# Gated cross attention and a quantised feed-forward: transposes from TensorE to the DMA queue, down projections two tiles late, and a written-out, reordered instruction stream

## The chip, the cores and the metric

One core of one Trainium2 chip. Times are device microseconds of one execution; lower is better. TensorE is written PE (matmuls) and PEld (its weight loads), VectorE is DVE, ScalarE is ACT, GpSimd is POOL, SyncE is SP.

## The reference

`x` is 8 batches of 256 x 512, the context likewise. Two stages follow one another:

```
xn = layernorm(x)                                   # rows of 512
theta = theta_w @ ctx + b;  phi = phi_w @ xn + b;  g = (g_w @ xn) + b     # latent 128
p  = softmax(theta^T phi)                           # 512 x 512 for each batch
tx = g applied to p;  h = relu(layernorm(tx over latent and time) * gamma + beta)
x  = x + tanh(g_xattn) * (out_w @ h + out_b + ctx)
# second stage, rows of 512, hidden 2048, each input quantised to 8 bits by its row's maximum,
# each weight to -1, 0, 1 by its mean absolute value
y  = layernorm(x);  q(z) = quantise(rmsnorm(z))
h  = silu(q(y) @ w1^T) * (q(y) @ w2^T);  out = x + tanh(g_ffn) * (q(h) @ w3^T)
```

## The kernel before

**Attention stage.** One step for each batch `i`. On TensorE `project(i)` makes theta, phi and g (L938, L944, L952); then `values(i - 1)` turns the four 128-column quarters of the older batch's probabilities (four 128 x 128 transposes each, L986) and contracts each with g (L980), with the output projection of batch `i - 2` (L967) between the first quarters; then the four score quarters of batch `i` (L1032: three matmuls each, since theta and phi are kept as a high and a low part) and two small matmuls with a matrix of 1/128 that average over the partitions (L998, L1002). VectorE takes row maxima (L603), low parts (L616), the statistics of the next batch (L589, L594), gamma (L664), the layer norm (L634) and the output add (L642). ScalarE makes the high parts (L466, L469), copies g and the turned quarters out of PSUM (L475, L452), does exponentials (L496) and relu (L447). GpSimd normalises the input (L287, `x_norm`) and the probabilities (L297, `normalise`), makes x + tanh(gate) * (ctx + bias) (`residual`, L272 and L276), and takes inverse roots (L264).

Beside it the three weights of the second stage (4 MB each) are loaded, summed in absolute value on ScalarE (L423), scaled and rounded on GpSimd (L283) and cut to their sign on ScalarE (L442).

The order of one TensorE step, with a wait of the next step's theta for the exponentials of this one:

```
def step(i, s, turn, before=True, older=True, weight=None):
    project(i, s, turn)        # theta waits exp_done 4*i - 3, phi 4*i - 2
    ...
        values(i - 1, 1 - s, out_proj if older else None)
    for c in range(TC):
        ...                    # scores of quarter c, mean_mm after c == 1
        var_mm(i - 1)
```

**Second stage.** 16 row tiles of 128 rows, two to a pair. For a tile, `up(t, k, c)` for c = 0 to 3 multiplies the turned, quantised input with 512 columns of w1 and of w2 (8 matmuls, L1074) into one of two pairs of PSUM banks. ScalarE: silu (L515), square with a sum (L524). VectorE: product (`hmul`, L782), maximum (L787), then the scale (L792 to L809). GpSimd: inverse root, rounding and writing of 8-bit values as bf16 in two halves (L360, L364). TensorE turns them (`turn_h`, 16 transposes, L1089), ScalarE copies them (L530), and `down(t - 1)` (16 matmuls, L1104) stands behind the up projections of tile t. The input of the next pair is prepared in the same way (`prep_*`), turned by `turn_x` (8 transposes, L1009) in the middle of a down projection and copied (L436). VectorE adds the residual (L815), SP stores the tile (L240).

Every engine runs its own instruction list; semaphores join them. The middle of both stages is a hardware loop on each engine (`Fori`), two batches or two tiles a turn. Between the stages, `values(B - 1)` and what follows it for the last batch stand between the up projections of tiles 0 and 1.

## Time and profile before

| | us |
|---|---|
| median of 3 runs | 359.27 (357.31 to 360.0) |
| the profiled execution | 357.35 |
| its span, first to last instruction | 355.6 |
| TensorE busy | 319.7 (90%) |
| VectorE busy | 250.6 (70%) |
| ScalarE busy | 242.8 (68%) |
| GpSimd busy | 209.7 (59%) |
| mean granted TensorE clock | 0.986 |

A busy share is a mean over both stages; the same engine may be full in one and half idle in the other. Matmuls overlap in the records, so the pitch from start to start is what one costs.

### The profile page before, as it was taken

To read this page: it belongs to the slowest core of one execution; us is meant where nothing else is said; L and a number is where in the kernel's file an instruction comes from. 1 tells how busy PE (TensorE), PEld (TensorE's weight loads), DVE (VectorE), ACT (ScalarE), POOL (GpSimd) and SP (SyncE) were. 2 spreads that over 40 slices of the span, in tenths; PEclk is the share of its full clock that TensorE was granted. 3 is DMA by queue.
4 is the path that set the end of the run, shared out by engine and by line. 5 is a ranking of instruction groups with operands and counts; after the bars stand their busy time and mean duration, and the time that the engine had idled before them with its cause. 6 is when DMAs were issued, how large, how long until landed. Compare 5 with 4: busy or idle time off the path is not lost.

```text
span 355.6 us, 5790 instructions
## 1 busy us (share of the span) xinstructions
PE 319.7 (90%) x1614; PEld 173.9 (49%) x1638; DVE 250.6 (70%) x608; ACT 242.8 (68%) x439; POOL 209.7 (59%) x237
## 2 busy tenths in 40 slices
PE   0999899899989996696999999999999999999955
PEld 0665556555656464342454454545544555455532
DVE  1438656756675699448888798788887987887560
ACT  1296767979797864785766687577776776667621
POOL 3768927795779565702756637646567275563530
PEclk9999999999999999899999999999999999999988
DMA  7977902545400000000000000000000000000000
GB/s 246 397 301 289 405 23 113 189 167 191 163 0 0 0 4 0 0 2 0 0 3 30 29 29 23 6 29 29 29 0 29 29 29 0 29 30 31 24 35 29
DMA packets 11471, 26.39 MB, mean 74 GB/s; under 512 B 1088, under 2 KB 1984, under 8 KB 10432
## 3 DMA queue, kind: packets, MB, share of 16 engines
q1 hardware_dynamic: 10352, 25.82, 19.0%
q10 hardware_dynamic: 1104, 0.40, 0.4%
q8 instruction: 6, 0.10, 0.1%
q14 instruction: 9, 0.07, 0.1%
HBM read 22.02 MB, written 4.19 MB: 74 GB/s over the span
## 4 chain that ended last, share of the span: by engine, by line
PE 38%; issue 19%; ACT 15%; DVE 14%; POOL 11%; DMA 2%; POOLq 1%; ACTq 0%; DVEq 0%
PE bank L1074 12%; PE bank L1104 8%; ACT prob L496 5%; POOL prob L297 5%; PE bank L980 5%; ACT wq L442 4%; PE bank L986 4%; PE bank L967 3%; POOL stage L364 3%; DVE m L787 2%; DMA g_w<-g_wt_dram 2%; PE bank L1089 2%; ACT stage L515 2%; PE bank L938 2%; POOL stage L360 1%
## 5 line engine op out<-in xcount | busy, mean ns | idle before, releaser
L1074 PE MATMUL bank<-wq,stage 128*128 128x512 bf16 x495 | 114.5, 379 | 4.4 <-ACT prob L496 1.3
L1074 PEld LDWEIGHTS bank<-wq,stage 128*128 128x128 bf16 x512 | 49.2, 98 | 60.6 <-DVE x L642 2.1
L515 ACT ACTIVATE stage<-bank,s 128x512 f32<-128x512 f32 x64 | 44.2, 690 | 43.1 <-PE bank L1074 28.8
L782 DVE SCALAR_TENSOR_TENSOR stage<-bank,s,stage 128x512 f32<-128x512 f32 x64 | 47.9, 749 | 27.4 <-ACT stage L515 17.7
L1104 PE MATMUL bank<-wq,stage 128*128 128x512 bf16 x249 | 60.2, 387 | 0.7 <-ACT stage L530 0.3
L524 ACT ACTIVATE stage<-stage 128x512 f32<-128x512 f32 x64 | 40.2, 629 | 5.3 <-DVE stage L782 5.3
L360 POOL TENSOR_SCALAR stage<-stage,hsc 128x1024 f32<-128x1024 f32 (+1 forms) x31 | 34.9, 1138 | 14.5 <-DVE hsc L807 14.5
L787 DVE TENSOR_REDUCE m<-stage 128x1 f32<-128x512 f32 x64 | 41.8, 675 | 0.0
L1104 PEld LDWEIGHTS bank<-wq,stage 128*128 128x128 bf16 x256 | 25.0, 99 | 30.2 <-issue 2.8
L297 POOL TENSOR_SCALAR prob<-prob,rsum 128x512 f32<-128x512 f32 x32 | 24.6, 783 | 21.4 <-DVE rsum L669 21.4
L530 ACT COPY stage<-bank 128x1024 bf16<-128x1024 bf16 x32 | 31.0, 1015 | 6.8 <-PE bank L1089 6.6
L264 POOL TENSOR_TENSOR fsc<-fsc,neghalf 128x2 f32<-128x2 f32 x16 | 11.2, 700 | 37.5 <-DVE fsc L736 19.9
L980 PE MATMUL bank<-probT,gs 128*128 128x512 f32 x64 | 32.5, 611 | 0.3 <-ACT probT L452 0.3
L364 POOL TENSOR_SCALAR stage<-stage 128x1024 bf16<-128x1024 f32 (+1 forms) x31 | 32.1, 1054 | 0.2 <-POOL stage L360 0.2
L452 ACT COPY probT<-bank 128x512 f32<-128x512 f32 x32 | 18.5, 584 | 15.0 <-PE bank L986 14.9
L1032 PE MATMUL bank<-ph,th 128*128 128x512 f32 x96 | 28.1, 429 | 0.0
L938 PE MATMUL bank<-c_sb,theta_w 128*128 128x512 f32 x32 | 17.5, 673 | 11.1 <-DMA g_w<-g_wt_dram 8.4
L496 ACT ACTIVATE prob<-bank,nmax 128x512 f32<-128x512 f32 x32 | 21.6, 685 | 6.3 <-DVE nmax L603 6.3
L423 ACT ACTIVATE wq<-stage 128x1024 bf16<-128x1024 f32 x24 | 25.4, 1058 | 0.0
L283 POOL TENSOR_SCALAR stage<-stage,winv 128x2048 f32<-128x2048 f32 x12 | 23.6, 1979 | 2.3 <-DVE winv L611 2.3
L986 PEld LDWEIGHTS bank<-ident,prob 128*128 128x128 f32 x128 | 15.6, 143 | 18.8 <-issue 17.1
L986 PE MATMUL bank<-ident,prob 128*128 128x128 f32 x128 | 19.8, 280 | 5.1 <-POOL prob L297 3.9
(100 smaller groups left out, 522.5 us busy)
## 6 DMA issues: line engine op xcount, KB each, us to landing
x_sb<-x_dram SPq DMA_DIRECT2D x8, 512.0 KB, 5.8
c_sb<-ctx_in_dram SPq DMA_DIRECT2D x8, 512.0 KB, 6.7
stage<-w1t_dram SPq DMA_DIRECT2D x4, 1024.0 KB, 13.9
stage<-w2t_dram SPq DMA_DIRECT2D x4, 1024.0 KB, 11.1
stage<-w3t_dram SPq DMA_DIRECT2D x4, 1024.0 KB, 6.1
out_dram<-stage SPq DMA_DIRECT2D x16, 256.0 KB, 2.0
gam<-gamma_dram SPq DMA_DIRECT2D x1, 256.0 KB, 6.2
bet<-beta_dram SPq DMA_DIRECT2D x1, 256.0 KB, 6.4
```

The lines of the kernel that those rows point to most:

```text
L297: nc.gpsimd.tensor_scalar(prob[:, c], prob[:, c], rsum[:, c:c + 1], 1.0, ALU.mult, ALU.mult)\
L360: nc.gpsimd.tensor_scalar(part, part, hsc[:, 5:6], ROUND, ALU.mult, ALU.add).then_inc(pool_chain, 1)
L364: nc.gpsimd.tensor_scalar(hq[:, lo:hi], h_sb[k][:, lo:hi], -ROUND, 1.0, ALU.add, ALU.mult).then_inc(hq_ready, 1)
L496: nc.scalar.activation(prob[:, c], b_sc[c][:, :], ACT.Exp, bias=nmax[:, c:c + 1], accum_out=esum[:, c:c + 1]).then_inc(exp_done, 1)
L515: nc.scalar.activation(sil[:, c % 2], bank[:, :], ACT.Silu, scale=s12[:, 0, k:k + 1])\
L524: nc.scalar.activation(junk, h_sb[k][:, c * 512:(c + 1) * 512], ACT.Square, accum_out=ssq[:, c:c + 1]).then_inc(sq_done, 1)
L782: V.scalar_tensor_tensor(h_sb[k][:, c * 512:(c + 1) * 512], bank[:, :], s12[:, 1, k:k + 1], sil[:, c % 2], ALU.mult, ALU.mult).then_inc(hm ...
L787: link.inc(V.tensor_reduce(m4[:, c:c + 1], h_sb[k][:, c * 512:(c + 1) * 512], AX_X, ALU.max, apply_absolute_value=True))
L980: return mm(b_gt[:, :], gs[:, s, c * P:(c + 1) * P], probT[:, c], start=c == 0, stop=c == TC - 1)
L986: last_tr = tr(b_pt[c % 2][:, tc * P:(tc + 1) * P], prob[:, tc, c * P:(c + 1) * P], ident[:, :])
L1074: last = mm(bank[:, :], xT[:, (k * KI + q) * P:(k * KI + q + 1) * P], wq[:, at:at + 512], start=q == 0, stop=q == KI - 1)
L1104: last = mm(b_dn[:, :], hT_sb[:, q * P:(q + 1) * P], wq[:, at:at + T], start=q == 0, stop=q == KF - 1)
```

## The change

Nearly the whole file is rewritten; the arithmetic on the tensors stays.

- All loops are written out; the helper `wait_apart` is gone.
- **Transposes of the second stage.** `turn_x` and `turn_h` leave TensorE and its PSUM banks. SP issues a DMA transpose of the whole turned input of a pair (128 x 1024 bf16) and of each half of a tile's hidden values (128 x 1024 bf16 each). Only the last tile is still turned by TensorE and copied by ScalarE and VectorE.
- **Late down projections.** `down(t - 2)` stands behind the up projections of tile t, not `down(t - 1)`. Two buffers for the quantised and for the turned hidden values; up projections go round three pairs of banks in place of two.
- **Attention order.** See the TensorE list below. Quarters 0 and 1 of the scores stand ahead of the turns of the older batch, and its values, the output halves of batch i - 2 and the other score quarters alternate. The small means of batch i - 2 stand behind theta and phi. Probabilities have two buffers, the turned quarters two of one quarter each. On ScalarE the first copy of a turned quarter stands behind the first exponential, the second behind the second, relu behind that.
- **Who does what.** x is loaded straight into its result buffer `x2`. VectorE normalises the input (`x_norm`) and adds the gated context (`residual`), which were GpSimd's; GpSimd makes only tanh(gate) * (ctx + bias), in place.
- Weights are treated in 24 pieces of 1024 columns, six ScalarE slots in each batch; maxima and squares of the hidden values are two of 1024 columns a tile in place of four of 512.

```diff
-            step(0, 0, 1, before=False, older=False)
-            step(1, 1, 1, older=False)
-            with pe.Fori(1, B // 2 - 1) as j:
-                step(2 * j, 0, j + 1, weight=j - 1)
-                step(2 * j + 1, 1, j + 1, weight=j - 1)
+            for i in range(B):
+                theta(i)                     # waits exp_done 4*i - 1
+                if i >= 2:
+                    mean_mm(i - 2, {3: 0, 5: 1}.get(i))
+                phi(i)
+                if i >= 2:
+                    var_mm(i - 2)            # waits dev_ready
+                g(i)
+                if i in (2, 4, 7):
+                    weight_total({2: 0, 4: 1, 7: 2}[i], i)
+                scores(i, 0)
+                scores(i, 1)
+                if i >= 1:
+                    turn_p(i - 1, 0)
+                    turn_p(i - 1, 1)
+                    values(i - 1, 0)
+                if i >= 2:
+                    out_proj(i - 2, 0)
+                scores(i, 2)
+                if i >= 1:
+                    turn_p(i - 1, 2)
+                    values(i - 1, 1)
+                if i >= 2:
+                    out_proj(i - 2, 1)
+                scores(i, 3)
+                if i >= 1:
+                    turn_p(i - 1, 3)
+                    values(i - 1, 2)
+                    values(i - 1, 3)
...
-            def turn_h(t):
-                for half in range(2):
...
-                        last = tr(b_hT[half][:, :].bitcast(BF16)[:, n * P:(n + 1) * P], hq[:, at:at + P], identb[:, :])
...
+            def turn_h(t):
+                for half in range(2):
+                    sp.wait_ge(hq_ready, 2 * t + half + 1)
+                    if t >= 2 and half == 0:
+                        sp.wait_ge(dn_done, t - 1)
+                    lo, hi = half * HF, (half + 1) * HF
+                    sp.dma_start_transpose(hT[t % 2][:, lo:hi].rearrange("p (n r) -> p n r", r=P), hq[t % 2][:, lo:hi])\
+                        .then_inc(hT_loaded[t % 2][half], 16)
...
+            for t in range(1, NT):
+                turn_h(t - 1)
+                if t % 2 == 0 and t // 2 + 1 < NU:
+                    turn_x(t // 2 + 1)
+                if t >= 3:
+                    store(t - 3)
...
+            for t in range(2, NT):
+                for c in range(FC):
+                    up(t, c)
+                down(t - 2)
+            down(NT - 2)
```

VectorE's and ScalarE's lists in one batch of the new kernel, from i = 2 on (without the weights):

```
VectorE: tx_mean(i-2), sum_inverse(i-1), low_part theta, tx_dev(i-2), low_part phi, tx_gamma(i-2), tx_var(i-2),
         x_stats(i+1), tx_norm(i-2), row_max 0, row_max 1, residual(i), x_norm(i+1), add_out(i-2, 0),
         row_max 2, add_out(i-2, 1), row_max 3
ScalarE: slot 0, theta_high, slot 1, phi_high, slot 2, g_copy, exp 0, p_copy(i-1, 0), exp 1, p_copy(i-1, 1),
         relu(i-2), slot 3, p_copy(i-1, 2), slot 4, exp 2, p_copy(i-1, 3), slot 5, exp 3
```

## Rows read from the trace of the kernel before

**Rows 1.** the page: busy time of each engine (share of span, instructions).

```profile
PE 319.7 (90%) x1614; PEld 173.9 (49%) x1638; DVE 250.6 (70%) x608; ACT 242.8 (68%) x439; POOL 209.7 (59%) x237
```

**Rows 2.** busy time (count) in five stretches; last: granted clock, DMA share, GB/s.

```profile
8.42:32.94 24.52, 24.23 (x100) 15.47 (x101) 12.93 (x29) 14.06 (x29) 19.18 (x23) 1.00 0.82 320
32.94:120.94 88.00, 80.75 (x346) 49.28 (x346) 57.41 (x130) 73.67 (x129) 66.75 (x70) 1.00 0.36 138
120.94:178.40 57.46, 47.33 (x215) 25.14 (x219) 41.79 (x107) 38.52 (x65) 28.56 (x31) 0.97 0.00 1
178.40:340.00 161.60, 159.55 (x922) 80.27 (x941) 132.17 (x330) 113.35 (x214) 89.69 (x99) 1.00 0.06 23
340.00:355.60 15.60, 7.89 (x35) 3.70 (x34) 4.52 (x10) 1.93 (x2) 3.27 (x3) 0.78 0.09 34
```

**Rows 3.** TensorE's timeline, batch 4: start, duration, line, operation [idle before].

```profile
67.68 1.98 PE L938 MATMUL bank<-c_sb,theta_w 128*128 128x512 f32 x4 [0.75 <-ACT prob L496]
69.50 1.88 PE L944 MATMUL bank<-xn,phi_w 128*128 128x512 f32 x4
...
73.86 0.65 PE L986 MATMUL bank<-ident,prob 128*128 128x128 f32 x4 [0.69 <-POOL prob L297]
74.34 1.02 PE L967 MATMUL bank<-hn,out_w 128*128 128x512 f32 x2
75.20 0.60 PE L986 MATMUL bank<-ident,prob 128*128 128x128 f32 x4
...
80.49 1.95 PE L1032 MATMUL bank<-ph,th 128*128 128x512 f32 x6
```

**Rows 4.** VectorE's timeline: low phi of batch 0, then batches 5 to 7.

```profile
14.79 0.75 DVE L616 SCALAR_TENSOR_TENSOR ph<-bank,biases,ph 128x512 fp32r<-128x512 f32 x1
...
89.05 1.18 DVE L634 SCALAR_TENSOR_TENSOR hn<-hn,tsc,bet 128x512 f32<-128x512 f32 x1 [1.36 <-POOL tsc L264]
90.16 1.27 DVE L589 BATCH_NORM_STATS2 xst<-x_sb 128x6 f32<-128x512 f32 x2
...
92.11 0.75 DVE L616 SCALAR_TENSOR_TENSOR th<-bank,biases,th 128x512 fp32r<-128x512 f32 x1
...
118.67 1.17 DVE L658 SCALAR_TENSOR_TENSOR tsc<-tsc,tmv 128x1 f32<-128x1 f32 x1
```

**Rows 5.** groups by line: shapes, count, busy us, mean ns, idle before.

```profile
L496 ACT ACTIVATE prob<-bank,nmax 128x512 f32<-128x512 f32 x32 | 21.6, 685 | 6.3 <-DVE nmax L603 6.3
L603 DVE TENSOR_REDUCE nmax<-bank 128x1 f32<-128x512 f32 x32 | 20.7, 682 | 1.1 <-PE bank L1032 1.1
...
L452 ACT COPY probT<-bank 128x512 f32<-128x512 f32 x32 | 18.5, 584 | 15.0 <-PE bank L986 14.9
```

**Rows 6.** TensorE's timeline over one pair of row tiles.

```profile
223.40 1.89 PE L1104 MATMUL bank<-wq,stage 128*128 128x512 bf16 x8
...
230.30 1.06 PE L1089 MATMUL bank<-identb,stage 128*128 128x128 bf16 x16
...
236.38 5.34 PE L1074 MATMUL bank<-wq,stage 128*128 128x512 bf16 x23
...
246.66 1.89 PE L1104 MATMUL bank<-wq,stage 128*128 128x512 bf16 x8
```

**Rows 7.** the page: DMA issues, KB each, median us to landing.

```profile
x_sb<-x_dram SPq DMA_DIRECT2D x8, 512.0 KB, 5.8
...
out_dram<-stage SPq DMA_DIRECT2D x16, 256.0 KB, 2.0
```

**Rows 8.** all engines' timeline: the last row tile.

```profile
337.21 3.62 PE L1104 MATMUL bank<-wq,stage 128*128 128x512 bf16 x16
...
341.68 0.91 DVE L917 TENSOR_SCALAR stage<-stage,hsc 128x1280 f32<-128x1280 f32 x1
...
352.18 0.75 DVE L815 SCALAR_TENSOR_TENSOR stage<-bank,dq,x 128x512 f32<-128x512 f32 x1 [7.58 <-PE bank L1104]
```

**Rows 9.** TensorE's timeline: its first up projection.

```profile
141.08 3.40 PE L1074 MATMUL bank<-wq,stage 128*128 128x512 bf16 x15 [1.26 <-ACT prob L496]
```

More of the change, by code:

```diff
@@ L381, in prep_root, with rounds @@
+            def rounds(k, lo, hi):
+                for p in range(lo, hi):
+                    weight_round(k, p)
             def prep_root(u):
@@ L401, in _, with prep_quant @@
-            pair(NT // 2 - 1, last=True)
+            def prep_quant(u):
+                pool.wait_ge(fqs_ready, u + 1)
+                for k in range(2):
+                    link.inc(G.tensor_scalar(y_sb[:, k], y_sb[:, k], fsc[:, 11, k:k + 1], ROUND, ALU.mult, ALU.add))
+                if u >= 1:
+                    pool.wait_ge(xT_loaded[(u - 1) % 2], 16 * ((u - 1) // 2 + 1))
+                link.wait(pool)
+                G.tensor_scalar(xq, y_sb.rearrange("p k t -> p (k t)"), -ROUND, 1.0, ALU.add, ALU.mult).then_inc(xq_ready, 1)
@@ new lines, in _ @@
+            square(1, 0)
+            relu(B - 1)
+            silu(1, 2)
+            silu(1, 3)
+            square(1, 1)
+            center(2)
+            for t in range(2, NT):
+                u = t // 2 + 2
+                silu(t, 0)
+                silu(t, 1)
+                square(t, 0)
+                silu(t, 2)
+                silu(t, 3)
+                square(t, 1)
+                if t % 2 == 1 and u < NU:
+                    center(u)
+            act.wait_ge(tail_a_ready, 1)
@@ L914, in _ @@
[L914 to L922 removed]
+            prep_max(1, 0)
@@ L1072, in up @@
+                if c == 0 and t % 2 == 0:
+                    pe.wait_ge(xT_loaded[(t // 2) % 2], 16 * (t // 4 + 1))
+                turned = xT[(t // 2) % 2]
+                for w, (bank, done) in enumerate(zip(up_banks(n), (up1_done, up2_done))):
                     for q in range(KI):
                         at = w * WCOLS + q * FF + c * 512
-                        last = mm(bank[:, :], xT[:, (k * KI + q) * P:(k * KI + q + 1) * P], wq[:, at:at + 512],
-                                  start=q == 0, stop=q == KI - 1)
+                        row = ((t % 2) * KI + q) * P
+                        last = mm(bank[:, :], turned[:, row:row + P], wq[:, at:at + 512], start=q == 0, stop=q == KI - 1)
@@ L1105, in down @@
                 last.then_inc(dn_done, 1)
-            def tile(t, k, u, before=True, prep=True, first=0):
-                if k == 0:
-                    pe.wait_ge(xT_ready, u + 1)
-                for c in range(first, FC):
-                    if c == 3 and before:
-                        turn_h(t - 1)
-                    up(t, k, c)
-                if before:
-                    down(t - 1, u + 1 if k == 1 and prep else None)
-            up(0, 0, 0)
-            up(0, 0, 1)
-            pe.wait_ge(xT_ready, 1)
```

1339 lines of the change are left out of this document (625 added, 714 removed).

## The prediction

> **What bounds the kernel now.** I read the page's busy shares first: TensorE is busy 90% of the span, every other engine 70% or less [rows 1]. Then the busy time by stage, cut where TensorE begins a new kind of work [rows 2]. Five stretches: the first two batches (8.4 to 32.9 us), batches 2 to 6 (32.9 to 120.9), batch 7 and the change of stage with the first two row tiles (120.9 to 178.4), the other 14 row tiles (178.4 to 340.0) and the end. Batches 2 to 6 take 88.0 / 5 = 17.6 us each, with TensorE busy 80.75 of 88.00. The row tiles leave TensorE 2 us idle in 161.6: they are at its limit. The change of stage holds 10.1 us of idle TensorE, the end 7.7. At the last-named place its granted clock falls too (0.78).
>
> TensorE's line of one batch gives the parts [rows 3]: 1.8 us from one projection to the next, 0.43 for four turns (73.86 to 74.34 is one quarter of the probabilities, 0.48 with its start), 0.86 for an output half (74.34 to 75.20) and as much for a quarter of the values. Six score matmuls take 1.95 with their end (80.49), 0.24 each from start to start, so 0.72 a quarter. Sum: 3 x 1.78 projections, 4 x 0.43, 4 x 0.86, 2 x 0.86, 4 x 0.72, and 0.5 for the small means = 15.6 us. So 2.0 of the 17.6 us are waits.
>
> For a pair of row tiles [rows 6]: 23.26 us from 223.40 to 246.66, in which there are 96 matmuls of 512 columns (24 of them, one without a record, take 236.38 to 241.56, so 0.216 each, 20.7 us) and 40 turns (16 take 1.06, so 0.066, 2.6 us). The two make up the whole period.
>
> **The change, part by part.** *Turns of the second stage go from TensorE to SP's DMA queue.* Per pair 40 turns leave TensorE (2.5 us, from 23.26 to 20.74), and their five copies leave ScalarE. A tile is then 32 x 0.216 = 6.91 us of up projections and 16 x 0.216 = 3.46 of down projection. What hides the transfers: the quantised half is written about 7.1 us into the next tile (scales 3.9, rounding 2.2, writing 1.0), and with the down projection two tiles late its first reader starts at 10.37 + 6.91 = 17.3. So the first half has 10 us, the turned input some 8. No transpose by DMA is in the trace. Its bounds: 2.0 us, the store of the same 256 KB [rows 7], and 5.8 us, the median load of 512 KB. I take 3 us, nearer to the store because it moves the same bytes. At 2.5 transfers a tile the queue is the limit only from 10.37 / 2.5 = 4.1 us each.
>
> *A rule beside it.* The Trainium skill (DMA: Bandwidth & Descriptors, Latency and other measured facts) gives 261 GB/s for a DMA transpose in one kernel; by that, an estimate, 256 KB are 1.0 us plus the fixed cost of a transfer. No row here shows it, and the sum doesn't use it.
>
> *Who else limits a tile then.* VectorE was busy 132.17 of 161.60 us [rows 2], 19.0 us of a 23.26 pair. The wider maxima (two of 1024 for four of 512) save about 0.4. It stays at 18.6 of 20.74, 90%, in order, with some 20 short waits on its own results: close, but with three bank pairs in place of two there is 3 us of slack behind TensorE. I take a tile at 10.37.
>
> *The attention batch is reordered.* A batch's end no longer waits for its last exponentials; the next batch's projections follow the values at once. But VectorE's order is new: between the low part of phi and the first row maximum stand gamma (0.67), the variance (0.1), the statistics of the next batch (90.16 to 92.11, 1.95) and the normalisation of the one before (1.1; 1.18 while GpSimd works) [rows 4]. And ScalarE copies the first turned quarter only after the first exponential. From the start of theta: phi ends at 3.9 (1.8 + 0.25 for the mean + 1.88), high part 0.69 (4.65), low part 0.67 (5.35), the four items 3.8 (9.15), row maximum 0.69 (9.9), exponential 0.66 (10.6), copy 0.59 (11.2), second exponential (11.85), second copy (12.4), relu 0.63 (13.0) (the passes of 512 columns on both engines: [rows 4, 5]). Only then the first output half, and behind it in TensorE's order: 0.86 output, 0.72 scores, 0.43 turns, 0.86 values, 0.86 output, 0.72 scores, 0.43 turns = 4.9 (17.9), the last copy 0.15 + 0.59 (18.7) and the last value matmuls 0.86: 19.6. A second place costs nothing more: the variance matmul stands before g and waits for VectorE until about 4.7, 1 us, but VectorE's list sets the later steps. I take 19.5 a batch against 15.6 of work: 1.9 worse than now. The copy of the other-batch quarter behind the first exponential is the point at which two score quarters ahead of the turns bite.
>
> *Input normalisation and residual go from GpSimd to VectorE.* Four passes of 512 columns a batch. Rows give 0.45 (the 1280-column pass, 0.91 us, scaled) to 1.18 (a pass with two SBUF inputs while GpSimd works) each, 1.8 to 4.7 us; I take 4.0. They stand behind the second row maximum (10.5) and before the first output add, which is thus done at 15.2 to 15.4. The second output half starts at 15.9. Hidden, with 0.5 us to spare.
>
> *What speaks against it.* A small VectorE step grew from 0.22 to 1.17 us while GpSimd was working [rows 4]. The Trainium skill (GPSIMD Engine Reference, Specifications) has the rule: GpSimd's SBUF interfaces are shared with VectorE, with contention for its 2-port modes and for two SBUF inputs. Both kinds move to VectorE here. The trace agrees, by that row; my sum takes the contended price, and the rival below doubles it.
>
> *Start.* Theta of batch 0 stays at 8.4. Batch 1 began at 18.5; it will wait for the third exponential, which stands behind the next statistics, two maxima, residual and normalisation. Low phi ends at 15.5 [rows 4]; 1.95 + 1.3 + 2.4 to 3.6 (four passes, free or at 0.9) + 0.69 + 0.66 make 22.5 to 23.7; I take 22.8. Batch 1, without an older batch's relu and output in it, takes 14.2 by the same walk: batch 2 starts at 37.0 (now 32.9).
>
> *Batch 7 and change of stage.* The input scales of the first pair stand behind the row maxima on VectorE, so they are ready at 20.9 into batch 7, quantised by GpSimd at 23, turned at 26: TensorE waits 6 us where it waited 1.3 [rows 9]. Behind it, batch 7's turns wait for two silus and a square on ScalarE, the mean of batch 7 for the product of up projection 3 (some 2.5 us), and up projection 6 for the pair's scales (1.3). I get 60 us from theta of batch 7 to the up projection of tile 2, of which 13.8 + 9.1 is TensorE's work and 15.6 the batch; now the same way, with one down projection and 24 turns more, takes 57.5 [rows 2].
>
> *The end.* Now: last up projection ends at about 337.2, the span 18.4 later [rows 8]. Two down projections (6.9) now stand in the gap that was idle. The chain behind the last up projection: scales 4.3 (341.68 less 337.4), VectorE's rounding 0.75 (1024 of the 1280 columns of that row), ScalarE's subtraction 1.05, wait for TensorE until 6.9, turns 0.6, copy 1.0, 16 matmuls 3.5, add 0.75, store 2.7, with the hand-overs 15.7. Gain 2.7.
>
> *Straight-line code.* The loops are written out. Loops on TensorE cost nothing that a row shows (idle 2 us in 14 tiles), so this is worth 0 either way; the bound is those 2 us.
>
> **The sum.** Batch 2 at 37.0; five batches at 19.5 and 0.5 more in two of them for the weight scale: 98.5, so batch 7 at 135.5; tile 2 at 195.5; 14 up projections 96.7 and 13 down projections 45.0: 337.2; the end 15.7: 352.9. The profiled execution took 357.35 for a span of 355.6, so 1.75 around it: 354.6, 0.8% under 357.35. The runs' median was 359.27, 0.5% above the profiled one. Two large amounts cancel: 17 us lost before tile 2 (195.5 against 178.4), 20 gained after it. A measurement of this kernel tells about 1% from no change.
>
> **Rivals.**
> *A, faster: the waits in the batch overlap.* If relu and the first copy are not held behind the exponentials as I count (VectorE runs ahead, the statistics fit in its waits), a batch costs what it does now, 17.6: five batches and batch 7 save 1.9 each, 11.4, giving 343; at TensorE's own 15.6 it is 354.6 - 6 x 3.9 = 331. For it: TensorE has only 15.6 us of work, VectorE some 14 to 16, ScalarE 13.4. Against: the engine orders are fixed, and I find no way round relu.
> *B, slower: the transposes are the bound.* From 4.1 us each the queue sets the tile. At 5 us a tile is 12.5, 14 tiles +30: 385; at 5.8, the load of x [rows 7], 14.5 and +58: 412. For it: every turn writes columns of 2 bytes across partitions, unlike any row here. Against: 10 us of cover, and DMA is otherwise nearly idle (0.06) in this stage [rows 2].
> *C, slower: GpSimd holds VectorE up.* The four moved passes and the small steps take twice the contended time where GpSimd rounds weights. It decides from 0.5 us a batch (the slack above) and 2 us a pair (20.74 - 18.6). At 1.5 us more a batch and 1 more a pair beyond that: 354.6 + 6 x 1.5 + 7 = 370. For it: VectorE at 90% in both stages.
>
> **Chances.** Forecast (350 to 361) 0.40, of it 0.13 below 353.8, 0.20 within 1%, 0.07 above; A 0.32; B 0.12; C 0.16. Faster 0.45, same 0.20, slower 0.35. The range reaches to A's middle and past C: 335 to 378; the forecast's own is 350 to 361.
>
> **What would show it.** In the profile after: theta of batch 2 near 37 and 19.5 us between thetas; before the first output half TensorE waiting for relu, before the first value matmuls for the copy; tiles of 10.4 us with TensorE busy throughout and SP's transposes landing within 3 to 4 us; up projection 0 waiting for a transpose for about 6 us; 15.7 us from the last up projection to the end. Wrong would be: thetas 17.6 apart or less (A), transposes above 4 us and TensorE waiting for them in every tile (B), VectorE busy without a gap and its two-input passes above 1.2 us (C).

## The result and the profile after

The changed kernel is slower: median 369.31 us of five runs (368.62 to 371.29) against 359.27, a ratio of 1.031 (95% interval 1.027 to 1.035). Its profiled execution took 371.29 for a span of 369.4, 2 us over its median. So the sum of the prediction is off by 16.5 us of span (369.4 against 352.9), the median by 14.7 from the forecast of 354.6. The profiled execution was the slowest of the five, its granted clock 0.943 where the other four had 0.953 or 0.954. Some executions of one kernel run longer at a lower granted clock than its others; ratios leave them out, and it matters below only for e9, whose profile is of such a run.

The page: busy shares, TensorE's granted clock in 40 slices of 9.2 us, DMA packets, and two issue rows (KB each, us to landing).

```profile
PE 316.3 (86%) x1317; PEld 161.5 (44%) x1334; DVE 266.7 (72%) x610; ACT 199.1 (54%) x349; POOL 182.6 (49%) x215
...
PEclk9999989879898999967898699999999999999999
...
DMA packets 51606, 36.45 MB, mean 99 GB/s; under 512 B 41216, under 2 KB 42112, under 8 KB 50560
...
out_dram<-stage SPq DMA_DIRECT2D x16, 256.0 KB, 2.3
stage<-stage SPq DMA_TRANSPOSE x38, 3.2
```

TensorE has 1317 matmul records in place of 1614 [rows 1], yet it was busy nearly as long and idle for longer: 369.4 - 316.3 = 53 us in place of 36. The clock row says where: in slices 6 to 23, the attention batches and the change of stage, ten stand at 8, 7 or 6; from slice 24 on, the row tiles, all are at 9.

Busy time by stage, cut at each theta projection, at the first up projection (173.16), at that of tile 2 and at the end of the last; columns as in [rows 2].

```profile
23.04:38.49 15.45, 14.07 (x61) 8.83 (x62) 8.05 (x17) 13.65 (x30) 4.89 (x7) 1.00 1.02 408
38.49:59.72 21.23, 17.89 (x72) 10.63 (x71) 15.04 (x32) 13.64 (x28) 10.30 (x11) 0.92 0.01 3
59.72:82.07 22.35, 19.17 (x69) 11.25 (x68) 15.02 (x28) 13.64 (x27) 10.30 (x11) 0.85 0.39 142
82.07:105.06 22.99, 17.67 (x72) 10.43 (x70) 13.47 (x32) 13.64 (x27) 9.22 (x11) 0.93 0.46 169
105.06:125.28 20.22, 17.70 (x70) 10.16 (x69) 14.94 (x28) 13.65 (x27) 10.31 (x11) 0.92 0.12 42
125.28:144.64 19.36, 16.18 (x70) 9.67 (x69) 15.24 (x28) 13.65 (x27) 11.55 (x12) 1.00 0.00 1
144.64:173.16 28.52, 19.56 (x71) 11.43 (x71) 18.04 (x48) 14.63 (x26) 15.94 (x19) 0.84 0.05 10
173.16:212.20 39.04, 30.93 (x102) 13.05 (x103) 25.30 (x60) 19.50 (x28) 16.44 (x18) 0.81 0.11 21
212.20:353.80 141.60, 140.86 (x644) 64.22 (x657) 122.68 (x296) 72.96 (x124) 88.25 (x99) 1.00 0.38 82
353.80:369.40 15.60, 11.36 (x64) 5.50 (x63) 8.48 (x18) 3.39 (x5) 1.18 (x2) 0.98 0.36 101
```

Tile 2 begins at 212.2 where it began at 178.4: 33.8 us are lost before it. From there to the end it is 157.2 us in place of 177.2: 20.0 are gained behind it. Of the five middle batches only one, batch 6, ran at the full clock (1.00), and it alone took what was forecast for each, 19.4; its four neighbours took 20.2 to 23.0 at 0.85 to 0.93.

TensorE's timeline of batch 5, and the first values of batch 4.

```profile
95.96 2.07 PE L917 MATMUL bank<-probT,gs 128*128 128x512 f32 x2 [4.87 <-ACT probT L449]
...
112.83 1.03 PE L910 MATMUL bank<-ident,prob 128*128 128x128 f32 x8
115.94 2.01 PE L917 MATMUL bank<-probT,gs 128*128 128x512 f32 x2 [2.07 <-ACT probT L449]
117.74 1.93 PE L930 MATMUL bank<-hn,out_w 128*128 128x512 f32 x2
118.77 1.59 PE L899 MATMUL bank<-ph,th 128*128 128x512 f32 x3
...
120.64 1.02 PE L917 MATMUL bank<-probT,gs 128*128 128x512 f32 x2
```

The eight turns end at 113.86; the first value matmuls wait 2.07 us for the copy of a turned quarter. And the two that wait take 2.01, the two of the next quarter, 4.7 us later, 1.02: behind the wait TensorE ran at the lower of its two clock levels (1.2 GHz in place of 2.4), through the output half too (1.93) and into the scores. The window over the first of these stretches gives the granted clock, 0.52:

```profile
115.94:118.77 2.83, 2.83 (x4) 1.00 (x5) 2.83 (x4) 2.67 (x5) 2.83 (x2) 0.52 0.27 68
```

VectorE and ScalarE in the same batch, and in batch 4.

```profile
92.78 1.15 ACT L410 ACTIVATE wq<-stage,neground 128x1024 bf16<-128x1024 f32 x1 [6.16 <-POOL stage L301]
...
93.87 0.16 DVE L647 RECIPROCAL winv<-wmt 128x1 f32<-128x1 f32 x1 [2.53 <-POOL stage L301]
...
111.03 1.28 DVE L562 BATCH_NORM_STATS2 xst<-x 128x6 f32<-128x512 f32 x2
...
113.92 1.28 DVE L591 TENSOR_REDUCE nmax<-bank 128x1 f32<-128x512 f32 x2
...
114.64 0.69 ACT L453 ACTIVATE prob<-bank,nmax 128x512 f32<-128x512 f32 x1 [2.40 <-DVE nmax L591]
...
115.31 0.57 ACT L449 COPY probT<-bank 128x512 f32<-128x512 f32 x1
...
116.72 2.52 DVE L576 TENSOR_SCALAR xn<-x,xnm,xrs 128x512 f32<-128x512 f32 x2
```

Read from the copy (115.31) backward: the quarter's four turns were done by about 113.4, but the copy is second in ScalarE's order, behind an exponential; that waits 2.40 us for a row maximum; the maximum (113.92) stands behind the next batch's statistics. That is the walk of the forecast: the copy ends 10.8 us into the batch, where 11.2 was reckoned. In batch 4 the same place is later still: VectorE waits 2.53 us to write the reciprocal of the weight scale, and ScalarE 6.16 us for a rounding, both on GpSimd's L301.

The change of stage and the row tiles on TensorE.

```profile
173.16 3.19 PE L974 MATMUL bank<-wq,stage 128*128 128x512 bf16 x7 [5.61 <-DMA stage<-stage]
...
204.45 1.72 PE L930 MATMUL bank<-hn,out_w 128*128 128x512 f32 x2 [2.01 <-ACT hn L445]
...
222.57 7.07 PE L974 MATMUL bank<-wq,stage 128*128 128x512 bf16 x31
...
232.93 7.07 PE L974 MATMUL bank<-wq,stage 128*128 128x512 bf16 x31
```

A tile is 10.36 us (222.57 to 232.93), 20.7 a pair against 23.26 [rows 6], without a wait.

### The profile page after: what moved, and what is told of

It reads as the page before. It is cut to its first block, busy times and chain, and to the rows that moved or that the text cites. A ratio compares the mean times of both kernels' runs of the same rounds, so it can differ in the third digit from the quotient of the medians.

```text
span 369.4 us, 4301 instructions
## 1 busy us (share of the span) xinstructions
PE 316.3 (86%) x1317; PEld 161.5 (44%) x1334; DVE 266.7 (72%) x610; ACT 199.1 (54%) x349; POOL 182.6 (49%) x215
## 2 busy tenths in 40 slices
DMA packets 51606, 36.45 MB, mean 99 GB/s; under 512 B 41216, under 2 KB 42112, under 8 KB 50560
## 4 chain that ended last, share of the span: by engine, by line
PE 66%; DVE 15%; ACT 8%; issue 4%; POOL 3%; DMA 3%; ACTq 0%; DVEq 0%
PE bank L974 28%; PE bank L993 14%; PE bank L917 7%; PE bank L930 5%; PE bank L872 4%; PE bank L878 3%; PE bank L899 3%; ACT prob L453 3%; DVE xst L562 2%; DMA g_w<-g_wt_dram 2%; PE bank L910 2%; DVE stage L704 2%; POOL xrs L276 2%; DVE ph L586 2%; ACT probT L449 1%
## 5 line engine op out<-in xcount | busy, mean ns | idle before, releaser
L477 ACT ACTIVATE xn<-stage 128x1024 f32<-128x1024 f32 x32 | 33.8, 1057 | 67.2 <-DVE stage L704 67.2
L471 ACT ACTIVATE stage<-bank,s 128x512 f32<-128x512 f32 x64 | 41.4, 675 | 18.8 <-PE bank L974 18.2
L709 DVE TENSOR_REDUCE m<-stage 128x1 f32<-128x1024 f32 x32 | 38.9, 1217 | 0.9
L332 POOL TENSOR_SCALAR stage<-stage,hsc 128x1024 f32<-128x1024 f32 x30 | 33.2, 1119 | 10.8 <-DVE hsc L727 10.8
L899 PE MATMUL bank<-ph,th 128*128 128x512 f32 x96 | 35.7, 497 | 1.8 <-ACT prob L453 1.4
L301 POOL TENSOR_SCALAR stage<-stage,winv 128x1024 f32<-128x1024 f32 x24 | 32.3, 1358 | 0.3 <-DVE winv L647 0.3
L410 ACT ACTIVATE wq<-stage,neground 128x1024 bf16<-128x1024 f32 x24 | 27.6, 1148 | 6.4 <-POOL stage L301 6.4
L338 POOL TENSOR_SCALAR stage<-stage 128x1024 bf16<-128x1024 f32 x30 | 30.8, 1043 | 0.0
L930 PE MATMUL bank<-hn,out_w 128*128 128x512 f32 x32 | 23.4, 822 | 6.6 <-ACT hn L445 4.6
L633 DVE SCALAR_TENSOR_TENSOR x<-bank,tg,x 128x512 f32<-128x512 f32 x16 | 12.0, 748 | 20.3 <-PE bank L930 20.3
L899 PEld LDWEIGHTS bank<-ph,th 128*128 128x128 f32 x96 | 19.0, 205 | 14.0 <-issue 9.8
## 6 DMA issues: line engine op xcount, KB each, us to landing
stage<-w1t_dram SPq DMA_DIRECT2D x4, 1024.0 KB, 13.8
```

What stands on the lines that cost most here:

```text
L301: G.tensor_scalar(piece(k, p), piece(k, p), winv[:, 0:1], ROUND, ALU.mult, ALU.add).then_inc(wround_done, 1)
L332: link.inc(G.tensor_scalar(part, part, hsc[:, 5:6], ROUND, ALU.mult, ALU.add))
L471: A.activation(sil[n % 3], up_banks(n)[0][:, :], ACT.Silu, scale=s12[:, u % 2, 0, k:k + 1]).then_inc(sil_done, 1)
L477: A.activation(junk, h_sb[t % 2][:, half * HF:(half + 1) * HF], ACT.Square, accum_out=ssq[:, half:half + 1]).then_inc(sq_done, 1)
L709: link.inc(V.tensor_reduce(m2[:, half:half + 1], h_sb[t % 2][:, half * HF:(half + 1) * HF], AX_X, ALU.max, apply_absolute_value=True))
L899: last = mm(b_sc[c][:, :], th[:, a, c * P:(c + 1) * P], ph[:, b], start=n == 0, stop=n == 2)
```

## Experiments

Each kernel is the changed kernel with the edit shown, or the experiment that its heading names with the edit shown; ratios are to the kernel before. Three dots in a diff stand for lines left out.

**e1: a column of its own for each weight's scale.** VectorE then need not wait for all roundings of the weight before.

```diff
-        winv = sb("winv", [P, 1])
+        winv = sb("winv", [P, 3])
...
-                if k >= 1:
-                    dve.wait_ge(wround_done, 8 * k)
-                V.reciprocal(winv[:, :], wmt[:, :])...
+                V.reciprocal(winv[:, k:k + 1], wmt[:, :])...
```

> Base: the changed kernel at 369.3 us. One change: the weight's inverse scale gets a column for each of the three weights, so that VectorE no longer waits, ahead of batch 4's first row maximum, until GpSimd has rounded all of the weight before. Theory (VectorE's and ScalarE's fixed order sets a batch): batch 4's wait before the first value matmuls falls from 4.9 to about 2.1 us, 366.5 in all; 365.5 if the clock also stays up there. Rival (GpSimd holds VectorE up in every batch, this wait is only one more of its kind): below 1 us, 368.5 or more.

Measured: 368.18 us, 1.025 (1.017 to 1.033), overlapping the change's own interval. VectorE's wait is gone, and batch 4 still takes 23.7 us. ScalarE's and TensorE's timelines of e1, batch 4:

```profile
91.40 1.15 ACT L410 ACTIVATE wq<-stage,neground 128x1024 bf16<-128x1024 f32 x1 [6.17 <-POOL stage L301]
94.23 2.08 PE L915 MATMUL bank<-probT,gs 128*128 128x512 f32 x2 [4.52 <-ACT probT L449]
```

Two waits on the same GpSimd pass stood side by side; taking one away leaves the other as long as it was (6.17 us for 6.16), a sign step of the weights in ScalarE's order ahead of the exponentials and the copies.

**e2: both copies ahead of the exponentials, relu behind them.** PE's order is left alone.

```diff
-                exp(i, 0)
                 if i >= 1:
                     p_copy(i - 1, 0)
-                exp(i, 1)
-                if i >= 1:
                     p_copy(i - 1, 1)
+                exp(i, 0)
+                exp(i, 1)
                 if i >= 2:
                     relu(i - 2)
```

> One change: ScalarE copies the first two turned quarters ahead of its first two exponentials, relu stays behind them. Theory of the order: the 2.1 us wait before the first value matmuls goes, but relu still stands behind the second exponential, so the first output half comes 0.5 to 1.0 us earlier in each of batches 2 to 7: 363 to 366. Rival (GpSimd and VectorE share what they read through, and that is what lengthens a batch): nothing to gain here, 369.

Measured: 360.15 us, 1.004 (1.000 to 1.007): 9 of the 10 us that the change had lost are back. TensorE's timeline of e2, batch 3:

```profile
65.68 1.13 PE L916 MATMUL bank<-probT,gs 128*128 128x512 f32 x2 [0.24 <-ACT probT L449]
68.32 1.10 PE L929 MATMUL bank<-hn,out_w 128*128 128x512 f32 x2 [1.51 <-ACT hn L445]
```

The copy costs 0.24 us in place of 2.07; the next in order, relu behind two exponentials, now costs 1.51. It falls behind the two value matmuls, and the output half after it runs at the full clock (1.10 for two matmuls). Four batches take 18.8 or 18.9; batch 4 still takes 24.2. The order alone is worth 0.6 us a batch: in batch 6, at the full clock in both kernels, 19.36 became 18.79. Batches 2, 3 and 5 gained 1.4 to 3.6, since their granted clock went from 0.85 to 0.92 up to 1.00. So of the 7.9 us that these four batches gained, 2.3 are the order's and the rest the clock's.

**e3: e2, and the turns ahead of the two score quarters.** This undoes one part of the change's attention order.

```diff
+                if i >= 1:
+                    turn_p(i - 1, 0)
+                    turn_p(i - 1, 1)
                 scores(i, 0)
                 scores(i, 1)
                 if i >= 1:
-                    turn_p(i - 1, 0)
-                    turn_p(i - 1, 1)
                     values(i - 1, 0)
```

> As the kernel before it in this call with the copies first, and in TensorE's list the two turned quarters of the older batch stand ahead of score quarters 0 and 1. Theory: TensorE reaches both before it has anything to wait for, so the place of the turns alone gives nothing: within 1 us of the kernel with the copies first. Rival (two score quarters ahead of the turns are the harm): 3 us or more below that kernel.

Measured: 361.10 us, 1.005 (1.001 to 1.009), no better than e2. TensorE's timeline and the window of e3, batch 3:

```profile
67.77 1.33 PE L929 MATMUL bank<-hn,out_w 128*128 128x512 f32 x2 [2.02 <-ACT hn L445]
68.30 2.07 PE L898 MATMUL bank<-ph,th 128*128 128x512 f32 x3
...
56.08:76.13 20.05, 17.58 (x69) 10.65 (x68) 14.83 (x28) 13.65 (x27) 10.31 (x11) 0.91 0.44 158
```

The first output half starts 11.7 us into the batch, as in e2: relu behind the two exponentials decides. What TensorE does earlier it only waits for longer there, 2.02 us in place of 1.51. Batches 2 and 6 take what they took in e2; batches 3 and 5 take 20.05 in place of 18.8, with the scores behind the longer wait at the lower clock (2.07 for three, 1.25 in e2).

**e4: the changed kernel with dummy matmuls in three waits.** 16, 8 and 72 extra matmuls of 128 bfloat16 columns fill TensorE's waits before the first values of a batch, before its first output half and before up projection 0. They add work whose result nobody reads.

```diff
                 if c == 0 and i >= 1:
                     pe.wait_ge(gam_done, i)
+                    if i < B - 1:
+                        keep_busy(16, b_tx)
                 pe.wait_ge(pT_ready, 4 * i + c + 1)
...
+            def keep_busy(n, bank):
+                for _ in range(n):
+                    mm(bank[:, 0:P], identb[:, :], identb[:, :], start=True, stop=True)
```

> The changed kernel with extra bf16 matmuls of 128 columns whose results nobody reads, in places where TensorE waits: 16 before a batch's first value matmuls, 8 before its first output half, 72 before the first up projection. They leave the order and all waits alone. Theory that the lower granted clock (0.943 against 0.986) behind these waits is a cost of its own: the clock rises to 0.97 or more and the time falls by 5 to 9 us, 360 to 364. Rival (the clock falls only where TensorE is not what is waited for): the extra matmuls cost or give at most 1 us, 368.5 to 370.5.

Measured: 362.60 us, 1.012 (1.004 to 1.021). More work, 6.7 us less time. Batch 5 of e4 can be laid beside that of the change:

```profile
110.94 1.12 PE L919 MATMUL bank<-probT,gs 128*128 128x512 f32 x2 [1.19 <-ACT probT L449]
...
119.38 1.88 PE L872 MATMUL bank<-c_sb,theta_w 128*128 128x512 f32 x4
```

The first value matmuls start 10.88 us behind theta in both: the dummies don't shorten what TensorE waits for. But from there to the next theta it is 8.44 us in e4 and 9.34 in the change (115.94 to 125.28), although e4 has 8 dummies more in it, and the two value matmuls take 1.12 in place of 2.01. The windows of e4 over batches 2 to 6 and over batch 7 up to the first up projection:

```profile
37.40:138.69 101.29, 89.72 (x465) 57.01 (x464) 73.20 (x148) 68.23 (x128) 51.69 (x56) 0.98 0.23 82
138.69:164.75 26.06, 21.99 (x168) 15.40 (x168) 18.03 (x48) 14.64 (x26) 15.95 (x19) 1.00 0.10 11
```

The other engines do the same work as in the change (VectorE 73.20 for 73.70, ScalarE 68.23 for 68.22); TensorE's granted clock is 0.98 in place of 0.92 and the five batches take 101.3 in place of 106.15. Theta of batch 7 to tile 2 takes 64.4 in place of 67.6. Together 8.0 us between the two profiled executions, 6.7 between the medians: what this filling gets back of the price of the lower clock. Batch 2 starts 1.1 us earlier as well, but that isn't the dummies' doing: the first of them stands in batch 2. There theta of batch 0 began 0.34 us earlier, and phi of batch 0 took 1.88 us in place of 2.39. In batch 4, where the wait stays at 3.96 us behind the dummies, the filling gains nothing (23.7 us for 23.0).

**e5: the order mended on three engines.** Copies and relu ahead of the exponentials on ScalarE; on VectorE the first output add and the third row maximum ahead of the residual, input normalisation last; GpSimd's last roundings of weight 0 a batch earlier, with e1's columns. TensorE's order is the change's.

```diff
VectorE:
                 row_max(i, 1)
+                if i >= 2:
+                    add_out(i - 2, 0)
+                row_max(i, 2)
                 residual(i)
-                if i + 1 < B:
-                    x_norm(i + 1)
...
-                if i >= 2:
-                    add_out(i - 2, 0)
...
-                row_max(i, 2)
...
                 row_max(i, 3)
+                if i + 1 < B:
+                    x_norm(i + 1)
GpSimd:
                 elif i == 3:
-                    rounds(0, 3, 6)
+                    rounds(0, 3, 8)
```

> Attention order mended as the walk along the lists says: ScalarE has both copies and relu ahead of the first two exponentials; VectorE adds the first output half and takes row maximum 2 before the residual, and normalises the next input last; the last rounded pieces of the first weight are made a batch earlier, with an inverse scale for each weight. Theory of the order: first value matmuls at 9.3 us into a batch, first output half at 10, so 16.9 to 17.5 us a batch in place of 19.4 (19.9 on a mean with batch 4), and with it less time at the lower clock: 342 to 350 in all. Rival (VectorE and GpSimd hold each other up, VectorE's sum of work sets the batch): not below 18.8 a batch, 356 or more.

Measured: 343.21 us, 0.956 (0.952 to 0.960): 26 us under the change and 16 under the kernel before. Batches 2 to 6 of e5:

```profile
37.38:122.48 85.10, 81.30 (x345) 48.80 (x344) 66.60 (x148) 68.29 (x128) 48.03 (x56) 1.00 0.30 104
```

17.0 us a batch, batch 4 no longer apart, clock 1.00 throughout.

**e6: e5, and relu's input and two row maxima ahead of the statistics on VectorE.**

```diff
+                if i >= 2:
+                    tx_norm(i - 2)
...
+                row_max(i, 0)
+                row_max(i, 1)
                 if i + 1 < B:
                     x_stats(i + 1)
...
-                    tx_norm(i - 2)
...
-                row_max(i, 0)
-                row_max(i, 1)
```

> The kernel before it in this call, and on VectorE the normalisation of the older batch and row maxima 0 and 1 also stand ahead of the next batch's statistics. Theory: 2 us less between the low part of phi and relu, so TensorE is bound by its own work but for the wait of the variance matmul: 16.2 to 16.8 a batch, 3 to 5 us below that kernel. Rival (bound elsewhere by then, the statistics being late for GpSimd's chain): within 1 us of it.

Measured: 346.14 us, 0.964 (0.960 to 0.968), 3 us slower than e5, against what I expected. The five batches take 86.5 in place of 85.1, the rest is lost in the change of stage. With copies and relu first nothing in the batch waits for the first maxima any longer; what comes later in return is the next batch's statistics, which GpSimd and the residual follow. GpSimd's and ScalarE's timelines of e6, batch 2, show where the 1.4 us begin:

```profile
49.10 4.26 POOL L301 TENSOR_SCALAR stage<-stage,winv 128x1024 f32<-128x1024 f32 x3
...
50.26 1.15 ACT L409 ACTIVATE wq<-stage,neground 128x1024 bf16<-128x1024 f32 x1 [1.15 <-POOL stage L301]
```

GpSimd's roundings start 11.6 us into the batch, behind its inverse root for the late statistics; in e5 they start at 9.6. ScalarE's sign step waits for them, and the copy of the third quarter stands behind it. The last value matmuls of batches 2 and 3 then wait 0.29 and 0.15 us for a copy, and in batch 4 the two small means come some 0.5 us late in all. Batches 5 and 6 take 16.84 and 17.21, as in e5 (16.86 and 17.20).

**e7: e6, with batch 7's scales for the first row tiles moved up on VectorE and GpSimd.**

```diff
                     prep_root(0)
-                    rounds(2, 0, 2)
+                    rounds(2, 0, 1)
                     prep_root_square(0)
-                    rounds(2, 2, 3)
                     prep_quant(0)
+                    rounds(2, 1, 3)
```

> The kernel before it in this call, and in batch 7 the scales of the first pair's input stand ahead of the residual and the second output add, its quantisation ahead of two pieces of weight rounding. Theory: the first up projection's wait of 5.6 us for the transposed input falls by about 3, and 2 to 4 us in all. Rival: the wait moves to the last batch's probabilities, which are late anyway: below 1 us.

Measured: 346.78 us, 0.966 (0.962 to 0.971), no gain. Up projection 0 no longer waits for its transposed input; just ahead of it, in e7:

```profile
145.94 2.08 PE L911 MATMUL bank<-probT,gs 128*128 128x512 f32 x2 [6.83 <-ACT probT L448]
```

The roundings that were pushed back hold ScalarE's sign step, and this the copy of batch 7's last quarter, for 6.8 us, the time that the other wait had taken.

**e8: the changed kernel, input normalisation back on GpSimd.** It separates rival C.

```diff
-                V.tensor_scalar(xn[:, o], x_tile(2 * b + o), xnm[:, o:o + 1], ...)
+                G.tensor_scalar(xn[:, o], x2[:, (2 * b + o) * T:(2 * b + o + 1) * T], ...)
```

> The changed kernel with the input normalisation back on GpSimd, nothing else. Theory of the order: those passes stand where VectorE has time to spare, so nothing to gain, 368 to 371; GpSimd's rounding moves 1.5 us later, which batch 4 may feel. Rival (moving them to VectorE is what costs, by contention and by load): 6 us or more below the changed kernel, 363 or less.

Measured: 368.68 us, 1.028 (1.022 to 1.035): no difference from the change that can be measured. VectorE was relieved of 11 us in batches 2 to 6 (62.2 busy for 73.7) and their time did not shrink (107.9 for 106.2). The difference is batch 4, where GpSimd's roundings come later, as expected (24.8 for 23.0); the other four take 83.1 and 83.2 us in all, and the first values start 10.88 us into batch 3 as before. The residual's passes stayed on VectorE.

**e9: e5 with the down projection one tile late instead of two.**

```diff
             for t in range(2, NT):
                 for c in range(FC):
                     up(t, c)
-                down(t - 2)
+                if t == 2:
+                    down(0)
+                down(t - 1)
```

> The kernel with the mended attention order (343.2 us), but the down projection is one tile late, as in the kernel before the change, in place of two; the transposes stay with the DMA queue. Theory (TensorE's turns could leave only because the second tile of delay covers the transfer): the first half is quantised 7.1 us into the next tile, lands 3.2 later at 10.3, and the down projection would start at 6.9, so TensorE waits 3.4 us in each of some 13 tiles: 387, up to 410 if the clock falls in these waits. Rival (the transfer is short enough by itself, the second tile of delay is spare): within 1 us a tile, 357 or less.

Measured: 1.089 (1.080 to 1.098). Three of the five runs took 389.46, 389.58 and 394.29 us, 46 to 51 over e5, the other two 397.64 and 405.70; the profile is of that of 397.64. TensorE's timeline of e9:

```profile
258.17 5.30 PE L988 MATMUL bank<-wq,stage 128*128 128x512 bf16 x16 [3.45 <-DMA stage<-stage]
...
278.27 7.07 PE L969 MATMUL bank<-wq,stage 128*128 128x512 bf16 x32
288.78 3.61 PE L988 MATMUL bank<-wq,stage 128*128 128x512 bf16 x16 [3.44 <-DMA stage<-stage]
292.23 7.07 PE L969 MATMUL bank<-wq,stage 128*128 128x512 bf16 x32
```

In 14 tiles the down projection waits for a transfer, 42 us in all and 3.4 at most by the view of waits. The tile shown takes 13.95 us (278.27 to 292.23) for 10.36; the seven from there to 373.67 take 13.6 each, and 14 x 3.3 = 46 is what the two fastest runs lost against e5. From 202.51 to 278.27 it is worse: the granted clock was 0.89, down projections behind the wait took up to 5.3 us in place of 3.6, and tiles up to 15.6. So the late down projection is what hides the transposes. Without it, and with nothing else changed, they cost more than the 20 us that the row tiles and the end gained.

**e10: e5, batch 7's scales earlier on VectorE only. e11: e10, and VectorE's and ScalarE's steps at the join of batch 7 and tiles 0 and 1 put in the order in which TensorE asks for them.**

```diff
e10, VectorE (what this moves is taken out behind the residual):
                 row_max(i, 2)
+                if i == B - 1:
+                    prep_square(0)
+                    prep_max(0, 0)
+                    prep_max(0, 1)
+                    fix_factors()
+                    prep_scale(0)
                 residual(i)
e11, VectorE:
+            tx_mean(B - 1)
             hmul(0, 3)
-            tx_mean(B - 1)
...
e11, ScalarE:
+            relu(B - 1)
             square(1, 0)
-            relu(B - 1)
```

> The kernel with the mended attention order, and in batch 7 VectorE makes the scales of the first pair's input ahead of the residual and the second output add; GpSimd's list stays. Theory: in the earlier kernel with both changed, a rounded piece that stood behind the quantisation held ScalarE up for 6.4 us and ate the gain; with GpSimd's list as it was, the wait of 6.1 us for the transposed input falls to 1 to 3: 339 to 341. Rival (what holds the first up projection is the end of batch 7 in any case): 342.5 or more.

> The kernel before it in this call, and where batch 7 meets tiles 0 and 1 VectorE takes the mean of batch 7 ahead of the product of up projection 3, product 4 and the layer norm ahead of the next pair's scales, and ScalarE takes relu ahead of the square. Theory: the waits of 1.9, 1.6 and 2.0 us there fall by some 4 in all, 335 to 338. Rival (each is followed at once by the next wait on the same chain): below 1 us.

Measured: e10 343.02 us, 0.960 (0.954 to 0.967), e5's time: up projection 0 still waits 5.9. GpSimd's passes over the first pair's input, in e5 and then in e10:

```profile
140.42 1.36 POOL L316 TENSOR_SCALAR stage<-stage,fsc 128x512 f32<-128x512 f32 x2 [1.50 <-DVE fsc L690]
...
138.29 2.34 POOL L316 TENSOR_SCALAR stage<-stage,fsc 128x512 f32<-128x512 f32 x2 [1.48 <-DVE fsc L690]
```

Counted from theta of batch 7, VectorE's scale came 1.2 us earlier in e10 (at 16.6 in place of 17.9 us), but GpSimd's two passes now fell beside the residual on VectorE (138.12 to 139.40) and took 2.34 us in place of 1.36; the quantised input was written at 20.2 in place of 20.4, and the transpose followed 3.4 us later in both. e11 342.06, 0.957 (0.950 to 0.963), at most 1 us better: its mean, its relu and its bank waits shrank, and 6.00 us appeared at the second output half, for an add on VectorE that stands in VectorE's list behind a maximum, the next pair's statistics and a product.

**e12: e5, with the turns ahead of the two score quarters (e3's edit).**

> The kernel with the mended attention order, with the two turned quarters of the older batch ahead of score quarters 0 and 1 in TensorE's list. Theory: the copies now come at once, so the place of the turns matters only by the 0.24 us wait in front of the first value matmuls, at most 1.5 us in all either way: 341.7 to 344.7. Rival (two score quarters ahead are good in themselves, since they give the maxima a start): 3 us or more slower, since maxima and exponentials come 0.9 us later in each batch.

Measured: 340.22 us, 0.951 (0.944 to 0.957), 3 us under e5, where I had expected 1.5 at most. It is the fastest of all. Of the 2.7 us between the profiled executions 0.8 lie before batch 2 (0.3 of them since theta of batch 0 began earlier) and 2.3 in batches 2 to 6; the change of stage gives 0.4 back. The runs of the kernel before beside the two stood at 359.3 and 357.8, so the ratio moved less than the time (0.956 to 0.951, with intervals that overlap); against e10, run beside it, it is 2.8 us. Windows of e12 over batches 2 to 6, and its timeline of batch 4:

```profile
36.60:119.37 82.77, 80.01 (x345) 48.70 (x344) 68.19 (x148) 68.60 (x128) 48.05 (x56) 1.00 0.32 109
```

```profile
76.28 1.07 PE L905 MATMUL bank<-ident,prob 128*128 128x128 f32 x8
77.11 1.64 PE L894 MATMUL bank<-ph,th 128*128 128x512 f32 x6
78.58 1.02 PE L912 MATMUL bank<-probT,gs 128*128 128x512 f32 x2
```

16.55 us a batch, against 17.0 in e5, whose first values start 0.24 us late for a copy. Here the scores (77.11 to 78.58) are the cover under which the copies are made, and no step in the batch waits but the variance matmul (0.45).

## Why the prediction was wrong

By the terms of its sum, in us of span (e12 beside it for what the order allows):

| term | forecast | after | e12 |
|---|---|---|---|
| batch 2 starts | 37.0 | 38.5 | 36.6 |
| batches 2 to 6 | 98.5 | 106.2 | 82.8 |
| theta 7 to tile 2 | 60 | 67.6 | 62.7 |
| 14 tiles | 141.7 | 141.6 | |
| the end | 15.7 | 15.6 | |

**Right.** The mechanism, in both directions. The row tiles: transposes 3.2 us to landing (taken: 3), a tile at 10.36 (10.37), TensorE idle 0.7 us in 141.6, the end to 0.1 us; rival B, the transposes as the bound, is ruled out as built, and e9 shows that the cover it was discounted for is real. The batch: the copy behind the first exponential, that behind the late row maximum; e2 removes just this and gives back 9 us, 0.6 a batch by the order and more by the clock that then stays up. Batch 6, the one at the full clock, took 19.4 where 19.5 was forecast. Up projection 0 waited 5.6 us for its transpose, forecast 6. Rival C, GpSimd as VectorE's brake: the measured 369.3 stands beside its 370, but by chance. Its sign, two-input passes above 1.2 us, did not come: the residual's took 677 to 1081 ns. The row tiles lost nothing. VectorE's other moved passes, those of the input, did take up to 1.3 us, but e8 shows that giving them back gains nothing.

In batches 2 to 6 the trace has VectorE's input normalisation at 543 ns at best, 1262 as the median and 1337 at most for the same 512 columns: 2.52 us for two passes beside GpSimd's roundings (batch 5), 1.00 where GpSimd had ended (batch 4). The residual's adds, with two inputs in SBUF, took 1.37 us for two beside the same roundings (batch 2), hardly more than at other times. The Trainium skill (GPSIMD Engine Reference, Specifications) has the rule that GpSimd's SBUF interfaces are shared with VectorE, with contention for VectorE's 2-port modes and for its passes with two SBUF inputs. The trace shows such a slowing for the first kind of pass moved here, little of it for the second, and no cost to the batch. The Trainium skill (DMA: Bandwidth & Descriptors, Latency and other measured facts) led to an estimate of 1.0 us plus a fixed cost for a transpose of 256 KB; the rows show 3.2 us.

**The step that failed: the sum priced waits at their length and matmuls at the full clock's durations.** "19.5 a batch against 15.6 of work", and "TensorE waits 6 us where it waited 1.3", had no term for what TensorE's clock does behind a wait. The warning stood in [rows 2]: 0.78 in the end, where TensorE idled 7.7 us. e4, which adds work in the waits and leaves what they wait for as it was, gives a size: 4.9 us in batches 2 to 6 and 3.2 in the change of stage, 8.0 in all between profiled executions; 6.7 between medians. That is about half of the error (16.5 and 14.7 us). It is not the clock's whole price: the dummies are work too, and e4 still ran at 0.82 in the change of stage.

**A second term mis-sized: the weight scale.** "0.5 more in two of them". Two batches were none the worse for it; batch 4 cost 4.3 us more than its neighbours (23.7 against 19.4 in e4). The forecast priced the small steps themselves and not VectorE's wait for GpSimd's last rounding of the weight before, nor the sign step queued in ScalarE behind the same rounding. e1 takes the first away and gains nothing sure; e5, with the rounding a batch earlier and both gone, has batch 4 at 17.1 like the rest. Against the forecast this is 3.7 us, less 0.9 that the other batches fell short of it. Part of the 3.7 is again the clock: batch 4 of e4 ran at 0.93, and its first value matmuls took 2.06 us.

**A third: the change of stage.** In e4 it took 64.4, the forecast was 60. Batch 7 up to the first up projection came out as forecast (26.06 in e4, against 26); behind it 4.4 us are missing. The window of e4 from there to tile 2:

```profile
164.75:203.10 38.35, 30.21 (x102) 12.99 (x103) 25.29 (x60) 19.50 (x28) 16.45 (x18) 0.82 0.11 21
```

The forecast had 13.8 + 9.1 = 22.9 us of TensorE's work here and left 11.1 for waits. TensorE was busy for 30.2 and idle for 8.1. So the waits in all were taken too long, though two of them were not in the list (2.02 for batch 7's relu, 1.95 for the second output half), and the matmuls too short. The last 8 matmuls of tile 1 took 3.3 us (199.81 to 203.10) where 8 take 1.7 at the full clock. How the 7.3 us of busy time above the forecast divide between the clock and small hand-overs isn't measured. e7, e10 and e11 show how little single moves give here: the released wait came back at another place of the same join (6.83 us in e7, 6.00 in e11), or the step before it grew (e10).

**A fourth: batch 1.** Batch 2 started at 38.5, forecast 37.0. Batch 1 took 15.45 us at the full clock, and 15.43 in e4, where the walk gave 14.2; that is 1.25 of the 1.5 us.

What the filling gives back 8.0, batches 2.8, change of stage 4.4, batch 2's start 1.5, less 0.2 in the tiles and the end: 16.5.

**Rival A** (faster, 331 to 343) did not occur in the changed kernel, for the reason given against it: the orders are fixed. Its times were reached with another order. Between its 15.6 us of TensorE's work a batch and the 17.6 of before lie e12's 16.55 and e5's 17.0; and these came from reordering alone, with every operation on the tensors kept. Two score quarters ahead of the turns are not shown to be the harm: with relu behind the exponentials, turning first gives nothing (e3 is not faster than e2). Only once relu stands ahead of the exponentials too, as in e5, does turning first pay, 3 us (e12). The changed kernel itself, with nothing but the turns first, was not run.

**What stays open.** Up projection 0 waits about 6 us in e5, e10, e11 and e12 alike, for one chain: VectorE's scale, GpSimd's passes, the transpose. No run had its input written much earlier: 20.4 us into batch 7 in e5, 20.2 in e10, 19.7 in e7. How to shorten it is open. Straight-line code was not run by itself. Not tried: e11 and e12 together, the residual back on GpSimd, and the transposing DMAs in the kernel before with its own attention order.

## What to carry to other kernels

Walk an engine's fixed order from the consumer backward, through each instruction that stands ahead of the one it waits for: a 0.6 us copy behind an exponential that waited for a maximum on another engine cost 9 us of 369, the smaller part by the wait itself and the larger by the lower clock behind it, and no share of busy time shows it. Where the walk finds waits in a TensorE-bound stage, add a term for the matmuls behind them, from rows at the lower clock. And when a wait goes, look at what waits for the same thing next to it (e1, e7): test the reordering as a set before judging it by single moves.

## What the runs showed that I had not expected

- Added work made the kernel faster: 24 dummy matmuls a batch and 72 before the first up projection took 6.7 us off it (e4), with the granted clock at 0.98 in place of 0.92 in the batches. After a wait of 2.07 us, two fp32 value matmuls took 2.01 us, at 1.2 GHz; two of the same shape took 1.02 at 2.4 GHz 4.7 us later. A wait that long did not always bring the lower clock at once: in e1's batch 5 the two behind a wait of 2.08 us took 1.12, and only the output half behind them 2.05.
- The 38 transposes of 256 KB were cut into small packets: 51,606 in the profile of after, where the one of before counts 11,471, and 41,216 of them under 512 bytes. By the difference, 40,135 / 38, that is some 1,050 packets a transpose, about 250 bytes each. DMA was busy 0.38 of the row tiles in place of 0.06 [rows 2], and stores slowed from 2.0 [rows 7] to 2.3 us, without any cost to the tiles.
